# Delta attention: unscaled keys shared by two blocks, new values scaled once more by VectorE

## The chip, the core and the metric

The kernel runs on one NeuronCore of one Trainium2 chip. It is one launch that computes four transformer layers; the time is the device time of the whole launch in microseconds (us), the median over several runs. The engines are TensorE (PE in the profile; PEld is its weight load), VectorE (DVE), ScalarE (ACT), GpSimd (POOL) and SyncE (SP), which issues the DMAs.

## What is computed

The change lies in the last layer's attention, a gated delta rule with 16 key heads, 32 value heads (two per key head) and a head size of 128, for 2 sequences of 512 tokens. The reference works chunk by chunk. For one chunk and one value head, with a state S (128x128), cumulated gate g and its last value g_last:

```
v_new = v_i - kcd_i @ S
out_i = (q_i * exp(g_i)) @ S + a_i @ v_new
S     = S * exp(g_last) + (k_i * exp(g_last - g_i)).T @ v_new
```

Then the output is multiplied by silu(z), normed, and projected. The factor exp(g_last - g_i) is one number per token and value head; it may be applied to the key row or to the row of v_new. The key itself is the same for both value heads of a key head.

## The kernel before, in words

The function `delta_and_looked_up` (from L1782) holds this attention. A chunk is 128 tokens, so a sequence has CH = 4 chunks. One iteration of the main loop works on one block w of W = 64: one key head h = w // 4 and one chunk c = w % 4, for the 2 sequences and the 2 value heads at once, so PR = 4 blocks of 128x128 side by side (B = 2 sequences, VPK = 2 value heads each). The state goes on from chunk to chunk inside a head, so the blocks of a head are serial, and the last chunk of a head (c = 3) grows no state.

The loop is a software pipeline written out by hand, one program per engine, with semaphores between them. In iteration w each engine works on several blocks:

- PE (L2341 to L2377), in this order: `recall(w-1)` (keys times state), `make_scores(w+2)`, `ask(w-1)`, `turn_values(w+2)`, `solve(w-1)`, then background part 0, `join_a(w)`, `grow_state(w-1)` (L2213), `close_a(w)`, `answer(w-1)` (L2205), `join_b(w)`, part 1, `close_b(w)`, `turn_out(w-2)` (L2222), part 2, `turn_keys(w+2)` (L2101), `join_c(w)`, `project_out(w-2)` (L2232), part 3, `close_c(w)`. The parts are projections of the next heads: iterations with c = 2 and c = 3 have three qkv parts (L2043), c = 0 has two, c = 1 has four z parts (L2053).
- ACT (L2519 to L2555): `make_decay` and `grow` (two exponentials, L2409 and L2415), `new_values(w-1)` (L2447: four scaled copies from PSUM, one per block, to `v_new`), copies of the inverse's pieces, squares, and last `make_keys(w+2)` (L2421: four copies from PSUM to `k_row`, each scaled by the gate K_LEFT of its block). In c = 1 it also does four silus of the next head, so that the exponential's table has to be loaded anew before the next `make_decay`.
- DVE (L2815 to L2851): `make_low(w+2)`, `make_right(w-1)`, `make_v0(w+2)` (L2650), `widen(w)`, `make_at(w+2)` (L2641), `close_wa(w)` (L2671), `make_qg(w+2)` (L2655), `copy_za(w)`, `carry(w-1)` (L2704), `gated(w-1)` (L2693, writes `xf`), the convolution of a later head (L2618, L2621), `copy_z_half`, `reduce(w-1)`, `add_out(w-2)` (L2725).
- POOL (L2601 to L2606): `substitute(w+2)` (L2577: the forward substitution of 16x16 blocks as 28 tiny multiplies and adds, L2585 to L2598), then `root(w-1)` (L2567) and `normed(w-1)` (L2573, writes `xnorm`).
- SP (L2008 to L2027): loads, `spread(w+2)` (v0 through DRAM to `l16`, what POOL's substitution starts from: L1970, L1976, L1984) and `gather(w+1)`.

The product that grows the state, L2218, takes per block its own scaled key `k_row[:, w % 4, r, :]` as the stationary operand and `v_new[:, r, :]`, 128 columns, as the moving one. `turn_out(w-2)` and `grow_state` share a PSUM bank (BR), `turn_values` and `turn_keys` another (BT), which is why `turn_values(w)` waits for the k_row copies of w - 1 (L2094).

Of the kernel before, what the change touches and what calls it, by code (L numbers as in the profile page):

```python
# [13 lines left out]
ALU = mybir.AluOpType  # L14
# [3 lines left out]
P = 128  # L18
# [3 lines left out]
TT = N // P  # L22
# [1759 lines left out]
def delta_and_looked_up(nc, ps, d, x, xn, norm, looked_up):  # L1782
# [19 lines left out]
    with Stage(nc, "a3") as s:  # L1802
# [49 lines left out]
        wa, wb, za, tb = (s.buf(n, [P, PR, HP]) for n in ("wa", "wb", "za", "tb"))  # L1852
        wc, z_half, t_half = (s.buf(n, [P, PR, P // 2]) for n in ("wc", "z_half", "t_half"))
        inv = s.buf("inv", [P, 2, PR, P])
        at, qg, v_row, k_row = (s.buf(n, [P, 4, PR, P]) for n in ("at", "qg", "v_row", "k_row"))
        state, rest, v_new = (s.buf(n, [P, PR, P]) for n in ("state", "rest", "v_new"))
        xf, sq, xnorm, out_t = (s.buf(n, [P, PR, P]) for n in ("xf", "sq", "xnorm", "out_t"))
        sums, var, rstd = s.buf("sums", [P, PR]), s.buf("var", [P, PR]), s.buf("rstd", [P, PR])

# [6 lines left out]
        def sems(*names):  # L1866
            return [s.sem(n) for n in names]
# [21 lines left out]
        (xf_ready, sq_ready, var_ready, rstd_ready, xnorm_ready, ot_psum, ot_ready, y_psum, added) = sems(  # L1889
            "xf_ready", "sq_ready", "var_ready", "rstd_ready", "xnorm_ready", "ot_psum",  # L1890
            "ot_ready", "y_psum", "added")
        (stored,) = sems("stored")
        (up_ready, silu_ready, gated_ready, down_done, f_added) = sems(
            "f_up_ready", "f_silu_ready", "f_gated_ready", "f_down_done", "f_added")
# [15 lines left out]
        def bank(n):  # L1910
            return ps[:, n, :].rearrange("p (r t) -> p r t", r=PR)
# [42 lines left out]
        with nc.Block() as block:  # L1954
# [82 lines left out]
            def _(pe):  # L2037
# [53 lines left out]

                def turn_values(w):
                    if w >= 1:
                        pe.wait_ge(krow_ready, PR * w)  # L2094
                    if w % CH == 0:
                        pe.wait_ge(qkv_ready, 4 * (w // CH) + 3 if w else 4)
                    for r in range(PR):
                        mm = pe.transpose(bank(BT)[:, r, :], chunk(w, 2 + r % VPK, r // VPK), ident[:, :])
                    mm.then_inc(vrow_psum, 1)
# [113 lines left out]
                def grow_state(w):  # L2213
                    if w % CH == CH - 1:
                        return
                    pe.wait_ge(vnew_ready, PR * (w + 1))
                    for r in range(PR):
                        mm = pe.matmul(bank(BR)[:, r, :], k_row[:, w % 4, r, :], v_new[:, r, :],  # L2218
                                       start=True, stop=True)
                    mm.then_inc(ds_psum, 1)  # L2220

                def turn_out(w):  # L2222
# [157 lines left out]
            def _(act):  # L2380
# [39 lines left out]

                def make_keys(w):  # L2421
                    act.wait_ge(krow_psum, w + 1)
                    for r in range(PR):
                        act.activation(k_row[:, w % 4, r, :], bank(BT)[:, r // VPK, :], ACT.Copy,
                                       scale=gate(K_LEFT, w, r)).then_inc(krow_ready, 1)

                def copy_tb(w):
                    act.wait_ge(a_psum, w + 1)
# [180 lines left out]
            def _(dve):  # L2609
# [74 lines left out]
                def make_right(w):  # L2684
# [4 lines left out]
                    for r in range(PR):  # L2689
                        dve.scalar_tensor_tensor(rest[:, r, :], bank(BR)[:, r, :], gate(K_NEG, w, r),  # L2690
                                                 v_row[:, w % 4, r, :], ALU.mult, ALU.add).then_inc(rest_ready, 1)

                def gated(w):  # L2693
                    dve.wait_ge(o_psum, w + 1)
                    if w % CH == 0:
                        dve.wait_ge(zs_ready, 4 * (w // CH) + 4)
                    if w >= 1:
                        dve.wait_ge(sq_ready, PR * w)
                        dve.wait_ge(xnorm_ready, w)
                    dve.scalar_tensor_tensor(xf[:, :, :].rearrange("p (b v) t -> p b (v t)", b=B),  # L2700
                                             bank(BO).rearrange("p (b v) t -> p b (v t)", b=B), float(P) ** -0.5,
                                             zs[:, w // CH % 2, w % CH::CH, :], ALU.mult, ALU.mult).then_inc(xf_ready, 1)
# [112 lines left out]
                for w in range(W + 2):  # L2815
                    late = w % CH == 2
                    if made(w + 2):
                        make_low(w + 2)
                    if made(w - 1):
                        make_right(w - 1)  # L2820
                    if made(w + 2):
                        make_v0(w + 2)
                    if made(w):
                        widen(w)
                    if made(w + 2):
                        make_at(w + 2)
                    if made(w):
                        close_wa(w)
                    if made(w + 2):
                        make_qg(w + 2)  # L2830
                    if made(w):
                        copy_za(w)
                    if made(w - 1):
                        carry(w - 1)
                        gated(w - 1)
                    conv(w, 0)
                    if late:
                        conv(w, 1)
                        conv(w, 2)
                    if made(w):  # L2840
                        copy_z_half(w)
                    if not late:
                        conv(w, 1)
                        conv(w, 2)
                        conv(w, 3)
                    if made(w - 1):
                        reduce(w - 1)
                    if late:
                        conv(w, 3)
                    if made(w - 2):  # L2850
                        add_out(w - 2)  # L2851
# [174 lines left out]
```

## Time and profile before

| what | value |
|---|---|
| median of 3 runs | 2029.11 us (2028.65 to 2031.85) |
| the profiled execution, its own time | 2028.85 us |
| span in that profile | 2027.0 us |
| PE busy over the span | 1843.1 us (91%) |
| DVE, ACT, POOL busy | 1287.5, 995.4, 1077.0 us |

The profile's page gives the busy time of each engine. A busy PE is not PE at its peak, since the ends of matmuls are modelled; and an engine with much idle time can still be in the path that sets the end. The main loop of the delta attention runs from about 950 us to the end. The chain of waits (followed back from the last instruction) names, piece by piece, what held the end; the view of waits adds up who waited for whom; the timeline shows single instructions with the idle time ahead of them in brackets.

### The profile page before, as it was taken

What the parts mean: (1) busy time and instruction counts of PE and PEld (TensorE: products, weight loads), DVE (VectorE), ACT (ScalarE), POOL (GpSimd) and SP (SyncE); (2) the same over time, 40 slices, a digit from 0 to 9 for tenths busy, and PEclk for the clock granted to TensorE, in tenths of its full rate; (3) what the DMA queues carried; (4) which work ended last, traced back from release to release, by engine and by line L of the source; (5) the groups of instructions that cost most, each with busy time, mean ns of one, the idle gap of its engine ahead of it and who ended that gap; (6) DMA issues with size and microseconds to landing.
All of it is one profiled execution on the core that took longest, in us unless ns stands there. A gap on an engine that the chain in (4) does not pass through costs nothing.

```text
span 2027.0 us, 45825 instructions
## 1 busy us (share of the span) xinstructions
PE 1843.1 (91%) x16855; PEld 1191.5 (59%) x16855; DVE 1287.5 (64%) x2490; ACT 995.4 (49%) x2433; POOL 1077.0 (53%) x2259
## 2 busy tenths in 40 slices
PE   7799997877899896898999999999999999999987
PEld 5422564432243574346777777777777777677775
DVE  2544564695578533627777777777777777777752
ACT  2375232215321452525656656665666566566643
POOL 0521222224100340126887787887878888888873
PEclk7899998998999796999999999999999999999999
DMA  6035422110010632202222222222222222222221
GB/s 157 1 116 156 108 46 53 52 62 1 1 44 7 176 116 88 40 14 56 53 53 64 64 54 54 64 63 55 49 60 54 53 64 64 54 53 64 44 45 32
DMA packets 231181, 124.42 MB, mean 61 GB/s; under 512 B 141360, under 2 KB 210513, under 8 KB 230705
## 3 DMA queue, kind: packets, MB, share of 16 engines
q1 hardware_dynamic: 225008, 111.20, 22.1%
q0 software_dynamic: 5952, 10.29, 2.2%
q8 instruction: 137, 2.24, 0.5%
q14 instruction: 84, 0.68, 0.1%
HBM read 87.94 MB, written 39.74 MB: 63 GB/s over the span
## 4 chain that ended last, share of the span: by engine, by line
PE 23%; POOL 20%; issue 6%; SPq 4%; ACT 3%; DMA 2%; DVE 2%; POOLq 0%; DVEq 0%; ACTq 0%
POOL a_term L2591 8%; POOL a_z L2595 8%; PE ps L2043 5%; PE ps L2053 3%; PE ps L2242 3%; SPq L1976 2%; POOL a_rstd L2567 2%; POOL a_xnorm L2573 2%; PE ps L2273 2%; DMA a_l<-a_v_dram 1%; SPq L1984 1%; PE ps L2229 1%; PE ps L2160 1%; PE ps L2209 1%; PE ps L2283 1%
## 5 line engine op out<-in xcount | busy, mean ns | idle before, releaser
L2591 POOL TENSOR_TENSOR a_term<-a_z,a_l 32x14 f32<-32x14 f32 (+6 forms) x896 | 342.8, 383 | 70.3
L2595 POOL TENSOR_TENSOR a_z<-a_z,a_term 32x14 f32<-32x14 f32 (+6 forms) x896 | 339.6, 379 | 70.2
L2621 DVE SCALAR_TENSOR_TENSOR a_qkv<-a_raw,a_taps,a_qkv 128x1024 f32<-128x1024 f32 x192 | 247.1, 1287 | 6.1
L2043 PE MATMUL ps<-all_xn,a_w_qkv 128*128 128x512 f32 x512 | 246.7, 607 | 0.0
L390 POOL DMA_INDIRECT f_rows<-a_row,a_slots x32 | 35.4, 1105 | 184.6 <-DVE a_of_tile L380 139.2
L2242 PE MATMUL ps<-a_out_t,a_w_out 128*128 128x256 f32 x512 | 130.7, 399 | 1.9 <-ACT a_out_t L2465 1.7
L2043 PEld LDWEIGHTS ps<-all_xn,a_w_qkv 128*128 128x128 f32 x512 | 89.2, 193 | 69.1 <-issue 67.3
L2386 ACT ACTIVATE a_raw<-ps 128x512 f32<-128x512 f32 x128 | 76.4, 598 | 108.2 <-PE ps L2043 107.5
L2053 PE MATMUL ps<-a_w_z,all_xn 128*128 128x256 f32 x512 | 122.6, 383 | 0.0
L2585 POOL COPY a_z<-a_l 32x256 f32<-32x256 f32 x64 | 27.1, 423 | 154.6 <-DMA a_l<-a_v_dram 154.4
L850 POOL DMA_INDIRECT f_sums<-a_y,a_xs x23 | 36.1, 1568 | 136.3 <-ACT a_y L799 133.4
L2242 PEld LDWEIGHTS ps<-a_out_t,a_w_out 128*128 128x128 f32 x512 | 93.8, 193 | 17.8 <-ACT a_out_t L2465 2.3
L2700 DVE SCALAR_TENSOR_TENSOR a_xf<-ps,a_zs 128x512 f32<-128x512 f32 x64 | 44.2, 690 | 91.0 <-POOL a_xnorm L2573 65.5
L2053 PEld LDWEIGHTS ps<-a_w_z,all_xn 128*128 128x128 f32 x512 | 93.6, 190 | 12.7 <-issue 1.2
L2650 DVE SCALAR_TENSOR_TENSOR a_v<-ps,a_gates,a_decay 128x128 f32<-128x128 f32 x256 | 71.6, 340 | 43.0 <-ACT a_decay L2409 43.0
L2450 ACT ACTIVATE a_v_new<-ps,a_gates 128x128 f32<-128x128 f32 x256 | 72.9, 367 | 45.7 <-PE ps L2192 45.7
L2635 DVE SCALAR_TENSOR_TENSOR a_low<-a_gc_rows,a_gates,a_floor 128x128 f32<-128x128 f32 x256 | 87.9, 403 | 1.6 <-DMA a_gc_rows<-a_g_dram 1.6
L630 PE MATMUL ps<-a_w,a_xt 128*128 x184 | 86.6, 593 | 0.6 <-ACT a_xt L779 0.6
L2567 POOL TENSOR_TENSOR a_rstd<-a_var,a_half 128x4 f32<-128x4 f32 x64 | 68.7, 1073 | 22.1 <-DVE a_var L2719 22.1
L772 ACT ACTIVATE a_probs<-ps 128x512 f32<-128x512 f32 x128 | 66.1, 602 | 23.9 <-PE ps L593 23.9
L2445 ACT ACTIVATE a_inv<-ps 128x512 f32<-128x512 f32 x64 | 38.3, 598 | 76.9 <-PE ps L2169 76.9
L2209 PE MATMUL ps<-a_v_new,a_at 128*128 128x128 f32 x512 | 74.8, 290 | 1.2 <-ACT a_v_new L2450 1.2
(331 smaller groups left out, 4304.7 us busy)
## 6 DMA issues: line engine op xcount, KB each, us to landing
a_gc_rows<-a_g_dram SPq DMA_DIRECT2D x64, 256.0 KB, 4.8
a_v_dram<-a_v SPq DMA_DIRECT2D x64, 256.0 KB
a_w<-in_f_w SPq DMA_DIRECT2D x24, 512.0 KB, 4.5
a_w_qkv<-in_a_w SPq DMA_DIRECT2D x16, 512.0 KB, 3.9
a_t_dram<-a_z SPq DMA_DIRECT2D x512, 8.0 KB
a_w_z<-in_a_w SPq DMA_DIRECT2D x16, 256.0 KB, 2.9
a_w_out<-in_a_wo SPq DMA_DIRECT2D x16, 256.0 KB, 3.1
a_v_off<-a_v SPq DMA_DIRECT2D x256, 4.0 KB
```

Source lines behind the costliest of these rows:

```text
L630: mm = pe.matmul(ps[:, bank + i % 2, :], xt[:, i % 2, k, :], w[:, bass.ds(e, 1), first + k * FF:first + (k + 1) * FF], start=k == 0, stop= ...
L2043: mm = pe.matmul(ps[:, to, :], w_qkv[:, k, mt * P:(mt + 1) * P], xn[:, k, b * T:(b + 1) * T], start=k == 0, stop=k == KC - 1)
L2053: mm = pe.matmul(ps[:, to, i * 256:(i + 1) * 256], xn[:, k, tt * P:(tt + 1) * P], w_z[:, k, :], start=k == 0, stop=k == KC - 1)
L2209: mm = pe.matmul(bank(BO)[:, r, :], at[:, w % 4, r, :], v_new[:, r, :], start=w % CH == 0 and r == 0, stop=r == PR - 1)
L2242: mm = pe.matmul(bank(BO)[:, B * m:B * (m + 1), :], w_out[:, v, m * P:(m + 1) * P], out_t[:, v::VPK, :], start=v == 0, stop=v == VPK - 1)
L2386: act.activation(raw[:, mt, b, TAPS - 1:], ps[:, of, :], ACT.Copy).then_inc(raw_ready, 1)
L2450: act.activation(v_new[:, r, :], bank(BR)[:, r, :], ACT.Copy, scale=gate(K_BETA, w, r)).then_inc(vnew_ready, 1)
L2567: pool.tensor_tensor(rstd[:, :], var[:, :], half[:, :], ALU.pow).then_inc(rstd_ready, 1)
L2591: pool.tensor_tensor(term[:, 0:j, j + 1:], z[:, 0:j, j:j + 1].broadcast_to([HP, j, n]), rows[:, j:j + 1, j + 1:].broadcast_to([HP, j, n]), ...
L2595: pool.tensor_tensor(z[:, 0:j, j + 1:], z[:, 0:j, j + 1:], term[:, 0:j, j + 1:], ALU.add).then_inc(sub_step, 1)
L2621: dve.scalar_tensor_tensor(to, rows, tap, to, ALU.mult, ALU.add).then_inc(conv_ready if j == TAPS - 1 else conv_step, 1)
L2635: dve.scalar_tensor_tensor(low[:, r, :], gc_rows[:, w % 2, r, :], gate(K_GC, w, r), floor[:, :], ALU.subtract, ALU.min).then_inc(low_ready, 1)
```

## The change

`make_keys` writes the keys unscaled, one ScalarE copy of 128x256 for the two sequences instead of four scaled copies of 128x128, and `k_row` shrinks from four blocks to two. A new VectorE step `make_left(w-1)` multiplies `v_new` (128x512, SBUF) by the gate K_LEFT, broadcast along each row, into a new buffer `v_left`, for every block but those with c = 3. It stands in VectorE's order between `make_at(w+2)` and `close_wa(w)`. `grow_state` uses the one key of a sequence as stationary operand and two blocks of `v_left`, 256 columns, as moving operand: two matmuls instead of four. It waits for `left_ready` and `krow_ready` as well.

```diff
-        at, qg, v_row, k_row = (s.buf(n, [P, 4, PR, P]) for n in ("at", "qg", "v_row", "k_row"))
-        state, rest, v_new = (s.buf(n, [P, PR, P]) for n in ("state", "rest", "v_new"))
+        at, qg, v_row = (s.buf(n, [P, 4, PR, P]) for n in ("at", "qg", "v_row"))
+        k_row = s.buf("k_row", [P, 4, B, P])
+        state, rest, v_new, v_left = (s.buf(n, [P, PR, P]) for n in ("state", "rest", "v_new", "v_left"))
...
                 def turn_values(w):
                     if w >= 1:
-                        pe.wait_ge(krow_ready, PR * w)
+                        pe.wait_ge(krow_ready, w)
...
                 def grow_state(w):
                     if w % CH == CH - 1:
                         return
+                    pe.wait_ge(krow_ready, w + 1)
                     pe.wait_ge(vnew_ready, PR * (w + 1))
-                    for r in range(PR):
-                        mm = pe.matmul(bank(BR)[:, r, :], k_row[:, w % 4, r, :], v_new[:, r, :],
-                                       start=True, stop=True)
+                    pe.wait_ge(left_ready, grown_before(w + 1))
+                    for b in range(B):
+                        mm = pe.matmul(bank(BR)[:, VPK * b:VPK * (b + 1), :], k_row[:, w % 4, b, :],
+                                       v_left[:, VPK * b:VPK * (b + 1), :], start=True, stop=True)
                     mm.then_inc(ds_psum, 1)
...
                 def make_keys(w):
                     act.wait_ge(krow_psum, w + 1)
-                    for r in range(PR):
-                        act.activation(k_row[:, w % 4, r, :], bank(BT)[:, r // VPK, :], ACT.Copy,
-                                       scale=gate(K_LEFT, w, r)).then_inc(krow_ready, 1)
+                    act.activation(k_row[:, w % 4, :, :], bank(BT)[:, 0:B, :], ACT.Copy).then_inc(krow_ready, 1)
...
+                def make_left(w):
+                    if w % CH == CH - 1:
+                        return
+                    dve.wait_ge(vnew_ready, PR * (w + 1))
+                    left = gates[:, K_LEFT * TT + w % CH:(K_LEFT + 1) * TT:CH, w // CH * VPK:(w // CH + 1) * VPK]
+                    dve.tensor_tensor(v_left[:, :, :].rearrange("p (b v) t -> p b v t", b=B),
+                                      v_new[:, :, :].rearrange("p (b v) t -> p b v t", b=B),
+                                      left.unsqueeze(3).broadcast_to([P, B, VPK, P]), ALU.mult).then_inc(left_ready, 1)
...
                     if made(w + 2):
                         make_at(w + 2)
+                    if made(w - 1):
+                        make_left(w - 1)
                     if made(w):
                         close_wa(w)
```

## Rows read from the trace of the kernel before

**Rows 1.** Iterations c = 2, 3, 0, 1: length, busy us of PE, PEld, DVE, ACT, POOL.

```profile
1293.50:1311.01 17.51, 17.51 (x215) 12.63 (x216) 12.40 (x28) 10.69 (x31) 12.54 (x29) 1.00 0.25 62
1311.01:1328.47 17.46, 17.46 (x216) 12.55 (x215) 14.00 (x32) 9.24 (x29) 14.90 (x36) 1.00 0.21 48
1328.47:1342.61 14.14, 13.72 (x200) 9.98 (x198) 9.97 (x22) 7.67 (x25) 12.14 (x29) 1.00 0.27 46
1342.61:1362.74 20.13, 18.83 (x228) 15.21 (x226) 14.93 (x31) 15.44 (x36) 17.10 (x42) 1.00 0.29 71
```

**Rows 2.** Waits, 1200 to 1950 us: who waited for whom, total us, times, longest.

```profile
POOL a_z L2585 <- DMA a_l<-a_v_dram: 35.1, 21, 3.3
PE ps L2229 <- POOL a_xnorm L2573: 7.0, 11, 1.4
```

**Rows 3.** Chain that ended last, 1275 to 1318 us: start, us, what.

```profile
1293.45 1.03 ACT a_k_row L2424 x4
...
1294.50 1.28 ACT L2409
...
1301.95 2.08 DMA a_l<-a_v_dram
```

**Rows 4.** The same chain, 1352 to 1415 us.

```profile
1368.20 1.09 PE ps L2218 x8
...
1379.35 1.06 PE ps L2180 x4
1380.41 0.86 PE ps L2087 x4
1381.27 0.89 PE ps L2203 x8
...
1404.78 2.50 DMA a_l<-a_v_dram
```

**Rows 5.** Groups by line and form, 952 to 1950 us: busy us, mean ns.

```profile
L2424 ACT ACTIVATE a_k_row<-ps,a_gates 128x128 f32<-128x128 f32 x232 | 66.1, 377 | 0.0
L2419 ACT ACTIVATE a_v_row<-ps 128x512 f32<-128x512 f32 x58 | 33.8, 583 | 0.0
L2441 ACT ACTIVATE a_wc<-ps 64x256 f32<-64x256 f32 x58 | 22.1, 381 | 20.1 <-PE ps L2160 19.3
L2655 DVE TENSOR_TENSOR a_qg<-a_qkv,a_grown 128x512 f32<-128x512 f32 x57 | 40.5, 710 | 0.0
```

**Rows 6.** Timeline, iteration with c = 1, from 1341 us: start, us, engine, line.

```profile
1343.46 0.27 POOL L2595 TENSOR_TENSOR a_z<-a_z,a_term 32x44 f32<-32x44 f32 x1
...
1347.68 0.68 DVE L2641 TENSOR_TENSOR a_at<-ps,a_decay 128x512 f32<-128x512 f32 x1
...
1348.19 1.16 PE L2218 MATMUL ps<-a_v_new,a_k_row 128*128 128x128 f32 x8
1348.34 0.29 DVE L2671 TENSOR_TENSOR a_wa<-ps,a_ident 128x128 f32<-128x128 f32 x1
...
1348.68 0.68 POOL L2595 TENSOR_TENSOR a_z<-a_z,a_term 32x44 f32<-32x44 f32 x1
```

**Rows 7.** Timeline at the end of an iteration with c = 1, from 1284 us: `turn_out`.

```profile
1284.89 0.63 PE L2229 MATMUL ps<-a_ident,a_xnorm 128*128 128x128 f32 x4 [0.37 <-POOL a_xnorm L2573]
```

**Rows 8.** Timeline, iteration with c = 3, from 1300 us.

```profile
1314.35 1.14 ACT L2450 ACTIVATE a_v_new<-ps,a_gates 128x128 f32<-128x128 f32 x4 [1.10 <-PE ps L2192]
...
1316.35 1.16 PE L2218 MATMUL ps<-a_v_new,a_k_row 128*128 128x128 f32 x8
...
1316.49 0.29 DVE L2671 TENSOR_TENSOR a_wa<-ps,a_ident 128x128 f32<-128x128 f32 x1 [1.43 <-PE ps L2115]
```

**Rows 9.** Timeline, iteration with c = 2, from 1284 us.

```profile
1296.89 1.14 ACT L2450 ACTIVATE a_v_new<-ps,a_gates 128x128 f32<-128x128 f32 x4
...
1298.88 0.97 PEld L2218 LDWEIGHTS ps<-a_v_new,a_k_row 128*128 128x128 f32 x8
```

**Rows 10.** Timeline of the last iterations, from 1990 us.

```profile
1999.62 1.16 PE L2218 MATMUL ps<-a_v_new,a_k_row 128*128 128x128 f32 x8 [0.85 <-ACT a_v_new L2450]
```

More of the change, by code:

```diff
@@ L1891, in delta_and_looked_up @@
             "ot_ready", "y_psum", "added")
+        (left_ready,) = sems("left_ready")
         (stored,) = sems("stored")
```

## The prediction

> **What bounds the kernel now.** The change touches only the main loop of the delta attention, so I first cut one head into its four iterations and read the busy times [rows 1]. In c = 2 and c = 3 PE has no idle time at all (17.51 of 17.51, 17.46 of 17.46 us); in c = 0 and c = 1 it idles 0.42 and 1.30 us. So PE has about 1.7 us of slack in a head of 69.24 us. POOL shows less busy time, but its instructions follow one another with short gaps. The view of waits shows its only real idle time: 35.1 us over 750 us, ahead of the substitution, until the DMA of l16 has landed, and also that PE waits 11 times for POOL's xnorm before `turn_out` [rows 2]. The kernel is thus held by PE and POOL in turn, and nothing is gained by relieving one alone.
>
> Next I read how they pass the lead on. The chain of waits leaves PE at the end of c = 1 and goes through ScalarE: the four k_row copies 1.03 us, the load of the exponential's table 1.28, the exponential `decay`, then v0 on DVE, the DMAs, and POOL's substitution [rows 3]. That is **path A**: after it the chain stays on POOL for three iterations and returns to PE at `turn_out` in the next c = 1. In other heads the chain stays on PE through c = 2 and c = 3, with `grow_state` on it (1.09 us), and reaches POOL's substitution only in c = 0, by another landing of the same DMA [rows 4]: **path B**. Both appear side by side in the same trace, so they are almost equally long.
>
> **The change, step by step.** I give each step's effect per head; about 14 heads run in this steady state.
>
> *ScalarE, k_row.* Four copies of 377 ns, started 1.03 us from first to next, or 1.15 to the end of the last, become one of 128x256. A copy of 64x256 takes 381 ns, one of 128x512 takes 583 [rows 5]. 0.38 is nearest in shape; the gain is 1.15 - 0.38 = 0.77 us, between 0.57 and 0.8. It is on the path once a head, ahead of the table load [rows 3]; `make_low` does not hold the load, since the chain runs there through k_row. In the other three iterations ScalarE waits for something else afterwards, so it costs and brings nothing there. What is late next is the DMA landing that POOL waits for, 3.3 us at most [rows 2], so the whole 0.77 is handed to POOL. Path A: -0.77.
>
> *PE, grow_state.* Four matmuls of 128 columns (two passes each, 8 instructions) become two of 256 columns (4 instructions). In place, the 8 take 1.09 us. In the middle of full-size work, 8 of the narrow form take 0.89 and 4 of the wide form 0.86; after small matmuls the wide ones take 1.06 [rows 4]. So the columns bind, not the count: I take 1.06, a gain of 0.03, between 0 and 0.23. Only path B has it, twice: -0.06. The Trainium skill (TensorE: Matmul & The Clock Gate, Back-to-back issue gap) gives a sustained spacing of 81 ns at 128 columns and 131 ns at 512, by which half as many at double width would be clearly cheaper: an estimate from it, 8 x 81 against 4 x at most 131 ns, saves at least 0.12 us a call. By it path B would be 0.24 shorter and the total about 1 us lower. The rows here, 111 and 216 ns, do not agree with it.
>
> *DVE, make_left.* A multiply of 128x512 with both inputs in SBUF: `make_qg` is the same shape and takes 710 ns on average [rows 5], and it holds DVE for some 0.65 us, as `at` does before `close_wa` (1347.68 to 1348.34 [rows 6]). It has to wait for `new_values`, and three things come of it.
>
> (1) In c = 3 v_new is complete at 1315.49, and DVE has 1.43 us of idle time before `close_wa` [rows 8]. The multiply ends near 1316.25, ahead of `grow_state` at 1316.35. Free for PE. In c = 2 v_new is complete at 1298.03 and `grow_state` starts at 1298.88 [rows 9]: 0.11 (the usual step to DVE) + 0.69 + 0.06 gives 1298.9, provided that DVE has finished `at` by 1298.1, which the 0.77 us from k_row takes care of. I take 0.05 of delay; without that cover it would be 0.36.
>
> (2) In c = 1 there is no cover: `at` and `close_wa` stand back to back, v_new has long been there, and `grow_state` starts at 1348.19 [rows 6]. Behind the multiply it starts at 1347.68 + 0.66 + 0.69 + 0.06 = 1349.09, 0.90 later. Queued behind it on PE are `close_a`, `answer`, `join_b`, and all up to `turn_out`; less the 0.03 this is +0.87. `close_wa` goes back 0.65, to 1349.0 to 1349.3, and is done before PE has finished the late `grow_state`. Before `turn_out` PE waits 0.37 us for POOL in the typical head [rows 7], so 0.50 of the 0.87 comes through, against a POOL that does not move. Call this **path C**: it takes path A's start and leaves POOL for DVE and PE one iteration earlier.
>
> (3) POOL shares something with DVE when both work in SBUF. The same POOL add of 32x44 takes 0.27 us alone and 0.68 us when `make_qg` runs over it [rows 6]: +0.41 for one such DVE instruction. `make_left` falls into the substitution in c = 3 and in c = 1, both on path A; in c = 2 it falls where POOL has some 2 us of wait ahead and is free. Per instance between 0 (an add that has just started long enough before) and 0.71 (the whole instruction). Here the Trainium skill (SBUF — State Buffer, SBUF: two separate sides) speaks against the change: a VectorE instruction with two SBUF inputs and a GpSimd one exclude each other for the whole instruction. I weigh that as a rival below; the sum goes by the row.
>
> **The sum per head.** Path A: -0.77 + 0.41 + 0.41 = +0.05. Path C: -0.77 + 0.41 (c = 3) + 0.50 = +0.14. Path B: -0.06 + 0.05 + 0.41 (the multiply of c = 1, in the last substitution before `turn_out`) = +0.40. With a third of the heads on B (5) and the others on the longer of A and C (9): 5 x 0.40 + 9 x 0.14 = 3.3 us. **The last iterations:** the parts end there, the chain passes twice more through k_row (-1.5), and in the last two growing steps the multiply lies bare between `new_values` and `grow_state` (which waits 0.85 for it already [rows 10]); one adds 0.25 because DVE waits for a DMA beside it, the other 0.8. Together -0.5. Sum: +2.8, and I round to +2.5 since some heads will change from B to C. The profiled execution took 2028.85 us, of which the span is 2027.0; it lies 0.26 below the median of 2029.11. 2028.85 + 2.5 = 2031.4, or **2031.6** against the median. A measurement of this kernel can tell 0.2%, 4.1 us, from no change; so the forecast is: no difference, leaning to slower.
>
> **The rivals.**
>
> *R1, slower: POOL is held for the whole multiply.* The mechanism is in (3), its price 0.71 instead of 0.41, twice on path A and once on B: A +0.65, B +0.70, so 14 x 0.67 = +9, less the end's 0.5: 2037.6. It decides from 0.5 us per instance. For it: the skill's rule, and POOL operations over 1 us in the 128x1024 convolutions. Against: 0.41 in the row, since POOL's own idle steps of 0.07 and the add's beginning overlap. Chance 0.15.
>
> *R2, slower: the k_row gain does not arrive.* Place: the turn from c = 1 to c = 2. If after k_row the table load or decay is held by `low`, or the earlier v0 only waits longer in SP's queue or for its DMA, 0.77 is missing and c = 2 loses its cover (+0.31). A +0.82, C +1.2, B +0.7: about +14, 2043. It decides from half of the 0.77. For it: landings of this DMA differ by half a microsecond (2.08 and 2.50 [rows 3, 4]). Against: each piece in the chain follows the one before without a gap. Chance 0.12.
>
> *R3, faster: the multiply costs POOL and PE little.* If the adds slip between, and PE's waits of c = 1 cover 0.87 more often (7.0 us in 11 waits [rows 2] is 0.64 on average): A -0.77, C -0.5, B -0.06 to -0.5 with the 0.23 of `grow_state` twice. 14 x 0.4 = -6: 2023. Chance 0.20.
>
> *R4: only balance.* That each path's changes cancel to within 0.1 us a head, 2029, is inside the forecast. That the change does not do what it says I give no chance of its own: the diff replaces instructions one by one, and none of the new ones can be left out.
>
> **The numbers.** Forecast with R4: 0.53; R1 0.15, R2 0.12, R3 0.20. The forecast's own spread, 2025 to 2038, puts some 0.11 of its 0.53 above 2033.2. Slower: 0.15 + 0.12 + 0.11 = 0.38; faster: 0.20; same: 0.42. The range goes from 2022 (R3) to 2041, near R2, whose upper part is left out.
>
> **What would show it.** Right: one k_row copy of 0.38 us; the idle time before L2585 at the turn to c = 2 down by up to 0.77; in c = 1 PE waits 0.9 us for a_v_left before `grow_state`, and no longer for xnorm before `turn_out`; POOL adds of some 0.7 us at two more places in each head; a `grow_state` of 1.0 to 1.1 us. Wrong: no wait for a_v_left in c = 1, POOL adds unaffected, or heads that are longer than 70 us by more than 0.5.

## The result and the profile after

The kernel after takes 2040.86 us, the median of 10 runs (2036.35 to 2051.86), against 2029.7 for the kernel before: ratio 1.0065 with a 95% interval of 1.0044 to 1.0087, that is 13.2 us more, between 8.9 and 17.7. (The ratios of this document weigh all runs of a set and are not the quotients of its medians; the two medians here differ by 11.2 us. Where an experiment's cost is given in us, it is its ratio taken of the kernel before.) The kernel after once more, in a later set of runs (the last experiment), gave 1.0052 (1.0033 to 1.0071). The forecast was 2031.6 and "no difference, leaning to slower"; it is slower by about five times the +2.5 us forecast. The median lies just inside the stated range, whose upper end of 2041 was drawn near the rival R2 and not from the forecast itself. The profiled execution was the fastest of the ten, 2036.35 us, so the traces below show less of the loss than the medians do.

From the profile's page of the kernel after, span and busy times:

```profile
span 2034.5 us, 45345 instructions
PE 1845.7 (91%) x16663; PEld 1179.5 (58%) x16663; DVE 1321.0 (65%) x2538; ACT 948.8 (47%) x2241; POOL 1092.7 (54%) x2259
```

ScalarE works 46.6 us less than before and DVE 33.5 more, as the diff says. POOL, whose code is not touched, is busy 15.7 us longer: the first sign that something holds it.

The four iterations of one head, windows of the kernel after; length, then busy us of PE, PEld, DVE, ACT, POOL, the granted clock of PE, DMA share and GB/s. They answer to [rows 1], each from PE's `make_scores` to the next: c = 2, 3, 0, then the c = 1 ahead of this c = 2 and the one behind this c = 0.

```profile
1298.19:1315.66 17.47, 17.47 (x210) 12.33 (x211) 13.11 (x29) 9.98 (x27) 13.08 (x30) 1.00 0.25 67
1315.66:1333.11 17.45, 17.45 (x212) 12.26 (x210) 14.62 (x33) 8.50 (x26) 15.04 (x34) 1.00 0.26 47
1333.11:1347.25 14.14, 13.72 (x200) 9.97 (x198) 9.68 (x22) 7.03 (x23) 11.49 (x27) 1.00 0.25 40
1277.54:1298.19 20.65, 18.87 (x225) 14.92 (x223) 15.45 (x32) 14.69 (x33) 17.62 (x42) 1.00 0.28 70
1347.25:1369.02 21.77, 18.88 (x224) 14.93 (x222) 15.88 (x32) 14.68 (x33) 18.59 (x44) 1.00 0.27 65
```

c = 2, 3 and 0 are as long as before, to 0.04 us: PE is never idle in the first two, before or after, and the shorter k_row copy can't change them. **What happens to a head happens in c = 1**: the six between 1200 and 1580 us took 20.13 to 20.81 us before and take 20.55 to 21.77 now.

What PE waits for there, timeline of the kernel after from 1276 us (start, us, engine, line; in brackets the idle time ahead and its releaser):

```profile
1278.14 0.38 ACT L2427 ACTIVATE a_k_row<-ps 128x256 f32<-128x256 f32 x1
...
1279.10 0.66 PE L2100 MATMUL ps<-a_ident,a_qkv 128*128 128x128 f32 x4 [0.44 <-DVE all_x L2736]
...
1282.60 0.68 DVE L2643 TENSOR_TENSOR a_at<-ps,a_decay 128x512 f32<-128x512 f32 x1
...
1282.73 0.45 PE L2117 MATMUL ps<-a_t_wide,a_v_off 32*32 32x32 f32 x32 [0.35 <-DVE a_t_wide L2665]
...
1283.20 0.67 DVE L2700 TENSOR_TENSOR a_v_left<-a_v_new,a_gates 128x512 f32<-128x512 f32 x1
1283.28 0.71 POOL L2593 TENSOR_TENSOR a_term<-a_z,a_l 32x44 f32<-32x44 f32 x1
...
1284.02 1.10 PE L2222 MATMUL ps<-a_v_left,a_k_row 128*128 128x256 f32 x4 [0.83 <-DVE a_v_left L2700]
1284.07 0.74 POOL L2597 TENSOR_TENSOR a_z<-a_z,a_term 32x44 f32<-32x44 f32 x1
...
1289.58 0.63 PE L2233 MATMUL ps<-a_ident,a_xnorm 128*128 128x128 f32 x4
```

The reader is to see four things: one k_row copy of 0.38 us; the multiply right behind `at`, and PE idle 0.83 us for it; two POOL steps of 32x44 that take 0.71 and 0.74 instead of 0.27, one beside the new multiply, one beside `make_qg` (this second one took 0.68 before, [rows 6]); and `turn_out` (L2233) that no longer waits for POOL's xnorm. In [rows 7] that wait was 0.37.

Waits, 1200 to 1950 us (total us, times, longest), against [rows 2]:

```profile
POOL a_z L2587 <- DMA a_l<-a_v_dram: 28.1, 24, 2.4
...
PE ps L2222 <- DVE a_v_left L2700: 11.6, 13, 1.2
```

POOL waits less for its DMA, 28.1 us for 35.1, but more often, 24 times for 21; and PE has a new wait of 11.6 us, larger than the 7.0 it had for xnorm (2.2 us, 3 times, now). The chain of waits, 1200 to 1360 us, shows the way that now ends last:

```profile
1201.30 1.05 POOL a_xnorm L2575
...
1208.43 0.69 DVE all_x L2736
1209.11 1.31 DVE a_low L2637 x4
1210.45 0.64 ACT a_decay L2413
1211.45 0.86 DVE a_v L2652 x3
1212.74 0.60 DVE a_at L2643
1213.35 0.61 DVE a_v_left L2700
1214.09 1.10 PE ps L2222 x4
...
1227.13 0.60 ACT a_inv L2447
1228.27 1.13 PE ps L2089 x4
...
1254.03 1.55 DMA a_l<-a_v_dram
```

POOL's xnorm in c = 0, DVE, the multiply, PE through c = 1 and on into c = 2 (from `a_inv` straight to PE, not through k_row), and only from c = 3 on the DMA and POOL. The k_row copy stands nowhere on it in this stretch. Over the 13 heads marked below, the chain passes through k_row at the turn to c = 2 in 8 heads of the kernel before and in 4 of the kernel after (in 4 of its repeat too).

**Where the time is, by stretch.** I mark the first and the fourteenth `turn_out` that stand in a c = 1, 13 heads apart. Timelines of the kernel before, then of the kernel after:

```profile
1005.84 0.63 PE L2229 MATMUL ps<-a_ident,a_xnorm 128*128 128x128 f32 x4 [1.07 <-POOL a_xnorm L2573]
...
1912.36 0.63 PE L2229 MATMUL ps<-a_ident,a_xnorm 128*128 128x128 f32 x4 [1.42 <-POOL a_xnorm L2573]
```

```profile
1009.49 0.63 PE L2233 MATMUL ps<-a_ident,a_xnorm 128*128 128x128 f32 x4
...
1921.53 0.63 PE L2233 MATMUL ps<-a_ident,a_xnorm 128*128 128x128 f32 x4
```

The 13 heads take 906.5 us before and 912.0 after, 0.42 us more each; in the repeat 912.5. So the steady state costs 5.5 to 5.9 us. The rest is at the two ends, which differ from execution to execution: 3.7 and 6.7 us later at the first mark (of the 6.7, 4.6 had arisen before PE's first instruction of this attention), and after the last mark 1.7 less and 4.7 more. The 13 heads are the best measure for a mechanism, the ratio for the whole kernel. I counted both, and also two things in the twelve heads behind the first mark: the mean idle time of PE in c = 1, by the step ahead of which it falls; and POOL's mean idle time ahead of its substitution, by the iteration in which that starts. The column of the 13 heads is one profiled execution each. In those of e1, e2, e4, e5 and e7, but not in the others, the granted clock fell to half for some 3 us inside the 13 heads (in e1, e4 and e5 in one c = 1 near 1357 us, which took 23.0 to 23.6 us), so differences of 2 us in that column decide nothing. The labels are those of the experiments below.

| kernel | ratio | 13 heads | PE idle in c = 1: turn_values / join_a / grow_state / turn_out | POOL idle in c = 2 / 3 / 0 / 1 |
|---|---|---|---|---|
| before | 1 | 906.5 | 0.89 / 0.18 / 0 / 0.48 | 2.52 / 0.10 / 0.19 / 0.31 |
| after | 1.0065 | 912.0 | 0.59 / 0.34 / 0.84 / 0.22 | 1.70 / 0.52 / 0.30 / 0 |
| e12, after again | 1.0052 | 912.5 | 0.61 / 0.33 / 0.84 / 0.27 | 1.87 / 0.49 / 0.32 / 0 |
| e1, no multiply | 0.9994 | 906.1 | 0.53 / 0.32 / 0 / 0.66 | 2.14 / 0.88 / 0.41 / 0.07 |
| e10, e1 in answer-first order | 0.9990 | 904.4 | 0.55 / 0.32 / 0 / 0.71 | 2.08 / 0.84 / 0.39 / 0.01 |
| e2, before + unread multiply | 1.0061 | 922.1 | 1.15 / 0.31 / 0 / 0.89 | 2.34 / 0.20 / 0.16 / 0.24 |
| e8, the same from PSUM | 1.0011 | 910.4 | 1.02 / 0.28 / 0 / 0.57 | 2.76 / 0.18 / 0.21 / 0.24 |
| e11, e2's multiply in c = 1 only | 1.0026 | 915.3 | 0.97 / 0.28 / 0 / 0.91 | 2.89 / 0.11 / 0.07 / 0.16 |
| e3, after, multiply from PSUM | 1.0047 | 910.5 | 0.54 / 0.33 / 0.84 / 0.22 | 2.28 / 0.71 / 0.42 / 0.08 |
| e4, after, answer first | 1.0034 | 913.5 | 0.66 / 0.30 / 0 / 1.10 | 1.90 / 0.49 / 0.24 / 0 |
| e5, both | 0.9996 | 906.5 | 0.48 / 0.33 / 0 / 0.83 | 2.12 / 0.83 / 0.43 / 0.03 |
| e6, before, answer first | 1.0025 | 906.7 | 0.89 / 0.21 / 0 / 0.54 | 2.38 / 0.15 / 0.22 / 0.38 |
| e7, e3 with the multiply before `at` | 1.0050 | 905.6 | 0.50 / 0.33 / 0.22 / 0.37 | 1.98 / 1.20 / 0.53 / 0.10 |
| e9, e7, answer first | 0.9986 | 907.1 | 0.56 / 0.37 / 0 / 0.74 | 2.07 / 1.01 / 0.39 / 0.05 |

### The profile page after: what moved, and what is told of

Same layout as the page of the kernel before. It is cut to its first block, busy times and chain, and to the rows that moved or that the text cites. A ratio compares the mean times of both kernels' runs of the same rounds, so it can differ in the third digit from the quotient of the medians.

```text
span 2034.5 us, 45345 instructions
## 1 busy us (share of the span) xinstructions
PE 1845.7 (91%) x16663; PEld 1179.5 (58%) x16663; DVE 1321.0 (65%) x2538; ACT 948.8 (47%) x2241; POOL 1092.7 (54%) x2259
## 4 chain that ended last, share of the span: by engine, by line
PE 27%; POOL 12%; DVE 8%; issue 5%; SPq 3%; ACT 3%; DMA 2%; DVEq 0%; POOLq 0%; ACTq 0%
PE ps L2045 5%; POOL a_term L2593 5%; POOL a_z L2597 5%; PE ps L2055 4%; PE ps L2246 3%; DVE a_qkv L2623 2%; PE ps L2211 2%; SPq L1978 2%; PE ps L2222 2%; PE ps L2277 2%; DVE a_low L2637 1%; DVE a_v L2652 1%; DMA a_l<-a_v_dram 1%; PE ps L2194 1%; PE ps L2233 1%
## 5 line engine op out<-in xcount | busy, mean ns | idle before, releaser
L2593 POOL TENSOR_TENSOR a_term<-a_z,a_l 32x14 f32<-32x14 f32 (+6 forms) x896 | 350.4, 391 | 70.3
L2460 ACT ACTIVATE a_sq<-a_xf 128x128 f32<-128x128 f32 x256 | 75.1, 297 | 0.0
```

Of the source, the lines that this page charges most:

```text
L2460: act.activation(sq[:, r, :], xf[:, r, :], ACT.Square, accum_out=sums[:, r:r + 1]).then_inc(sq_ready, 1)
L2593: pool.tensor_tensor(term[:, 0:j, j + 1:], z[:, 0:j, j:j + 1].broadcast_to([HP, j, n]), rows[:, j:j + 1, j + 1:].broadcast_to([HP, j, n]), ...
```

## The experiments

Theory: PE and POOL are two paths of the same length that meet at `turn_out` in c = 1, and the change lengthens both, PE's by a bare wait for v_left and POOL's by the time in which the multiply holds it, while k_row's gain is on neither (e2 corrects this last point). Rivals: the gain is real and the multiply eats it; or only one of the two costs counts.

**The gain's half alone (e1).** No `make_left`; `grow_state` multiplies `v_new` itself, so the factor exp(g_last - g_i) is left out of the state.

```diff
-                    pe.wait_ge(left_ready, grown_before(w + 1))
...
-                                       v_left[:, VPK * b:VPK * (b + 1), :], start=True, stop=True)
+                                       v_new[:, VPK * b:VPK * (b + 1), :], start=True, stop=True)
...
-                    if made(w - 1):
-                        make_left(w - 1)
```

> The changed kernel without its multiply: one unscaled key copy, the wide matmul takes v_new itself (so the factor exp(g_last - g) is left out of the state). Theory L (a combined path: PE enters c = 2 through a_zs, not through k_row, so the 0.77 us of the copies are mostly not on the path; the 13 us come from the multiply, which makes PE wait 0.9 us in c = 1 and holds POOL): 1 to 4 us below the kernel before. Rival G (the key copies were really on the path in every head and the gain of 0.77 us is there, only more than eaten up by the multiply): 8 to 11 us below.

Measured: 0.9994 (0.9978 to 1.0009), so 1.2 us below, inside the theory's 1 to 4, and the rival's 8 to 11 lie outside the interval. No gain that can be told, though four copies had become one and eight matmul instructions four. Waits of this run, 1200 to 1950 us:

```profile
POOL a_z L2586 <- DMA a_l<-a_v_dram: 40.0, 26, 3.6
...
PE ps L2232 <- POOL a_xnorm L2574: 7.7, 11, 1.8
```

POOL waits longer and more often than before (35.1 us, 21 times), and the table says where. In c = 2 v0 and `at` do stand 0.76 us earlier against PE's work. But the next one, in c = 3, then waits 0.88 us instead of 0.10 for its own DMA, whose source v0 is made by PE's side, and PE has no slack in c = 2 and c = 3 [rows 1]. POOL's starts, counted from PE's `make_scores` of c = 2 (means of the twelve heads), show it at once: the substitution of c = 2 starts at 10.56 us before and at 9.73 in e1, the next one, of c = 3, at 27.31 and 27.24. Of 0.83 us only 0.07 is left: what was saved is returned one iteration later. The chain passes through k_row in 1 of the 13 heads of e1, against 8 before. In c = 1 PE waits 0.36 less for the keys and 0.32 more before `join_a` and `turn_out`.

**The cost's half alone (e2, e8).** The kernel before, with the multiply in its place on DVE, and nobody reads `v_left`. In e2 it reads v_new from SBUF, as the change does; in e8 its first input is a PSUM bank of the same shape (the second part of the diff is e8 against e2).

```diff
+                    if made(w - 1):
+                        make_left(w - 1)
                     if made(w):
                         close_wa(w)
...
-                                      v_new[:, :, :].rearrange("p (b v) t -> p b v t", b=B),
+                                      bank(BK).rearrange("p (b v) t -> p b v t", b=B),
```

> The kernel before plus the multiply in its place on VectorE; nobody reads v_left and PE does not wait for it (close_wa behind it still goes back). It has the cost on VectorE and GpSimd alone. Theory L: two POOL stalls of 0.4 us a head, +3 to +7 us against before, about half of the change. Rival C (contention between VectorE and GpSimd is the whole cost): +12 us or more. Rival W (PE's wait before grow_state is the whole cost): within 2 us of before.

> The kernel before plus a multiply that nobody reads, like the one that cost 12 us, in the same place and with the same wait, but its first input is the scores in PSUM instead of v_new in SBUF. Same time on VectorE, one SBUF input instead of two. Theory L2: the 12 us go to 0 to +2 us. Rival O: +8 to +13 us.

Measured: e2 1.0061 (1.0037 to 1.0085), 922.1 us for 13 heads; e8 1.0011 (0.9993 to 1.0029), 910.4. By the ratios an unread multiply costs as much as the whole change, 12.4 us, at the lower edge of the rival C that I had set against my own +3 to +7; and most of it (10.2 of the 12.4 us, and 11.7 of the 15.6 in the 13 heads) disappears with one input in PSUM, at the same duration of the multiply. Timeline of e2, then of e8, the multiply in c = 1 and the POOL step beside it:

```profile
1282.60 0.29 POOL L2596 TENSOR_TENSOR a_z<-a_z,a_term 32x50 f32<-32x50 f32 x1
...
1282.90 0.68 DVE L2699 TENSOR_TENSOR a_v_left<-a_v_new,a_gates 128x512 f32<-128x512 f32 x1
1282.96 0.72 POOL L2592 TENSOR_TENSOR a_term<-a_z,a_l 32x44 f32<-32x44 f32 x1
```

```profile
1281.57 0.68 DVE L2699 TENSOR_TENSOR a_v_left<-ps,a_gates 128x512 f32<-128x512 f32 x1
1281.64 0.28 POOL L2592 TENSOR_TENSOR a_term<-a_z,a_l 32x50 f32<-32x50 f32 x1
```

0.68 us on DVE in both; POOL's step (32x44 and 32x50, which alone take 0.25 to 0.29) takes 0.72 beside the one and 0.28 beside the other. Most of the cost is thus not DVE's time but what the multiply takes from POOL. What e8 still shows in its 13 heads, 3.9 us, was not followed up; `close_wa` stands later there as well.

k_row's gain is not wholly without use, though. POOL's substitution of c = 3 starts, on the same scale as above, at 27.31 us before, at 28.07 in e2 (at 27.52 in e11 below, without the multiplies of c = 2 and c = 3) and at 27.27 in the kernel after. With the multiply that runs beside the substitution begun in c = 2, the next one comes 0.76 late, and with the shorter k_row it is in time again. It agrees that the 13 heads of the kernel after, 912.0, are 10.1 us shorter than e2's although PE waits for v_left there (0.78 a head); the ratios of the two, 1.0065 and 1.0061, do not show it, so over the whole kernel this stays open.

**One of the three multiplies (e11).** As e2, but only in the iteration with c = 1.

```diff
-                    if w % CH == CH - 1:
+                    if w % CH != 0:
                         return
```

> The kernel before with the unread multiply from SBUF, only in the iteration in which c = 0's values are scaled (it runs in c = 1, beside the substitution that ends at turn_out). With it in all three iterations the time was 1.0061 [1.0037, 1.0085]. Theory (POOL's adds are held 0.4 to 0.5 us per multiply on POOL's path, once a head here instead of twice or three times): a third to a half of it, +4 to +7 us. Rival 1 (only this one counts, since it is the last ahead of turn_out): +12. Rival 2 (only those of c = 2 and c = 3 count; in c = 1 POOL's substitution has slack, or closing w_a late is what costs): 0 to +2.

Measured: 1.0026 (1.0012 to 1.0039), +5.3 us, 915.3 for 13 heads: 8.8 of the 15.6 us that all three cost in this stretch, by the ratios 5.3 of 12.4. So the dose counts, and the multiply of c = 1, the last ahead of `turn_out`, bears about half. The substitution that is running when c = 1 begins takes, from its first to its last instruction, 15.13 us instead of 14.57.

**From PSUM in the changed kernel (e3).** beta is taken into the gate once, and the multiply reads the same bank that `new_values` reads.

```diff
+                dve.tensor_tensor(kind(K_LEFT), kind(K_LEFT), kind(K_BETA), ALU.mult).then_inc(g_step, 1)
...
-                                      v_new[:, :, :].rearrange("p (b v) t -> p b v t", b=B),
+                                      bank(BR).rearrange("p (b v) t -> p b v t", b=B),
```

> The changed kernel, but the multiply takes its first input from PSUM (the solve's result times a gate that already holds beta times exp(g_last - g)) instead of v_new in SBUF; same place, same wait for v_new, same size. It then has one SBUF input, like make_at, over which POOL was hardly late. Theory L: the POOL stalls at the multiply go, PE's wait of 0.9 us in c = 1 stays: +5 to +9 us against before. Rival C: back to before or below it (0 to -3). Rival W: +12 us, no change.

Measured: 1.0047 (1.0032 to 1.0063). Waits of e3, 1200 to 1950 us:

```profile
PE ps L2222 <- DVE a_v_left L2700: 10.4, 12, 1.2
...
PE ps L2233 <- POOL a_xnorm L2575: 1.8, 3, 0.7
```

POOL is free again and early, and PE is late at `turn_out` by itself: it waits for v_left in every head and for xnorm in three. With POOL relieved, the kernel still loses 9.5 us by its ratio, just over the +5 to +9 expected, and 4.0 us in the 13 heads. That this is PE's bare wait is shown by e5 below, which covers the wait and loses nothing.

**Answer first (e4).** PE's order becomes join_a, answer, close_a, grow_state, join_b, so that two steps which don't need v_left cover the multiply.

```diff
-                    if made(w - 1):
-                        grow_state(w - 1)
+                    if made(w - 1):
+                        answer(w - 1)
                     if made(w):
                         close_a(w)
-                    if made(w - 1):
-                        answer(w - 1)
+                    if made(w - 1):
+                        grow_state(w - 1)
```

> The changed kernel with another order on PE: join_a, answer, close_a, grow_state, join_b. answer (1.09 us) needs v_new alone and covers the multiply; it also covers the wait of 0.42 us for close_wa in c = 0. Theory L: PE's wait in c = 1 goes, POOL's stalls stay: 0 to +5 us against before. Rival C: +12 us. Rival W: 2 to 8 us below before, since 0.42 us a head of PE's idle time goes as well.

Measured: 1.0034 (1.002 to 1.0049), 6.9 us, where 0 to +5 had been expected. Timeline of e4 in c = 1:

```profile
1281.02 1.16 PE L2211 MATMUL ps<-a_v_new,a_at 128*128 128x128 f32 x8
...
1282.76 1.13 PE L2222 MATMUL ps<-a_v_left,a_k_row 128*128 128x256 f32 x4
...
1287.47 0.63 PE L2233 MATMUL ps<-a_ident,a_xnorm 128*128 128x128 f32 x4 [0.91 <-POOL a_xnorm L2575]
```

The wait for v_left is gone, and 0.91 us of waiting for POOL stands in its place: the other path, held by the multiply, is now the long one.

**Both (e5).**

> Both remedies at once: the multiply reads PSUM, and PE does answer ahead of close_a and grow_state. Theory L2 (after the first four runs: POOL is held about 0.5 us by each multiply with two SBUF inputs, which alone explains the 12 us of the unread multiply; PE's bare wait of 0.9 us in c = 1 is a second, separate cost of up to 9 us on a path that does not pass k_row; each alone is as large as both together, because the slowest path counts): both gone, so 0 to -6 us against before. Rival O (the cost is VectorE's own time: any instruction of 0.67 us in that place costs it): +5 us or more still.

Measured: 0.9996 (0.998 to 1.0013). Timeline of e5:

```profile
1280.16 0.67 DVE L2700 TENSOR_TENSOR a_v_left<-ps,a_gates 128x512 f32<-128x512 f32 x1
1280.23 0.25 POOL L2593 TENSOR_TENSOR a_term<-a_z,a_l 32x44 f32<-32x44 f32 x1
...
1285.94 0.63 PE L2233 MATMUL ps<-a_ident,a_xnorm 128*128 128x128 f32 x4 [0.33 <-POOL a_xnorm L2575]
```

Each remedy alone leaves 7 to 9.5 us (their intervals overlap that of the kernel after, so the ratios alone don't prove either of them a help); the two together leave nothing. That is how two parallel paths behave, and not how two costs in a row do.

**The same order without the change (e6), and the multiply ahead of `at` (e7, e9).** e6 is the kernel before with e4's order; e7 is e3 with `make_left` ahead of `make_at`; e9 is e7 with e4's order.

> The kernel before with only PE's order changed (join_a, answer, close_a, grow_state, join_b), which covers PE's wait of 0.42 us for close_wa in c = 0. Theory L2 (POOL's path is as long as PE's and is untouched): 0 to -3 us. Rival P (the kernel before is bound by PE alone, so its idle time counts in full): -5 to -6 us.

> The multiply from PSUM, and ahead of make_at instead of behind it; PE's order as in the changed kernel. In c = 1 it should end 0.66 us earlier, so that PE's wait before grow_state shrinks from 0.9 to 0.25 us. Theory L2: 0 to +4 us against before, 5 us or more below the multiply from PSUM behind make_at (which was 9.5 above). Rival O: no better than that one, +8 to +11 us.

> The kernel after with all remedies: multiply from PSUM with a premultiplied factor, issued ahead of make_at, and PE's order answer, close_a, grow_state. Theory (two costs on parallel paths: POOL held by the multiply's SBUF inputs, and PE's bare wait in c = 1; both gone here): 2024 to 2030 us, within 0.2% of before, as the run with the two remedies (0.9996). Rival (placing the multiply first delays at, the state's narrow matmuls and with them the substitution's input, a third path of its own, as the run with only the early PSUM multiply suggests, 1.0050): 2034 us or more. Sign to look at in the profile: from at of c = 2 to v0, and POOL's wait for a_l, each longer by up to 0.7 us under the rival.

Measured: e6 1.0025 (1.0009 to 1.0041), e7 1.0050 (1.0025 to 1.0075), e9 0.9986 (0.9971 to 1.0001). The first two are misses: 0 to -3 us had been expected of e6 and 0 to +4 of e7, and e7's 10 us are what rival O (any instruction of that length in that place costs it) had foretold. In the profiled execution of e7 the 13 heads take 905.6 us and PE waits 0.22 for v_left instead of 0.84, as hoped, and this execution took 2027.87 us; but only three of the eight runs lie there (2025.6 to 2028.5), the others at 2035.4 to 2042.7, and none of those was profiled. The mean granted clock parts the two groups: 0.955 to 0.959 in the three, 0.949 to 0.953 in the five. So rival O fits the ratio and not the profile; what lowers the clock in one execution and not in the next is left open. e6's heads take 906.7, as before, and by its ratio it is 5 us slower all the same. e9 has the lowest ratio of the kernels that keep the change, and can't be told from the kernel before or from e5.

**k_row's gain again, with answer first (e10).**

This is e1, whose state leaves the factor out, in e4's order.

> The gain's half (single key copy, wide matmuls, no multiply; the state leaves out the factor left) with PE's order answer, close_a, grow_state. Theory (the key copy's 0.77 us is never on the slowest path, whatever PE's order): between the kernel before (1.000) and the kernel before with that order (1.0025), so 2028 to 2034 us. Rival (the order frees POOL's path, and then k_row's saving shows): 2020 to 2024 us, 0.3% below before.

Measured: 0.9990 (0.9977 to 1.0003), 904.4 us for 13 heads. Not the 0.3% of the rival: by the ratio it is 2 us of the 10.8 that 14 times 0.77 would be, and POOL again waits 0.84 us in c = 3. That it lies below e6, whose order it has, speaks for some of the gain; its interval, which holds 1.000, leaves this open.

**The kernel after once more (e12).**

> The kernel after unchanged, on the same chip as the three others, to have its median and interval beside theirs and a second profiled execution. Theory: 1.0044 to 1.0087 again, +9 to +18 us, PE in c = 1 waiting some 0.8 us for a_v_left, POOL's period in c = 3 17.1 to 17.2 us. Rival (the difference was that chip's or that set of runs'): within 0.2% of before.

Measured: 1.0052 (1.0033 to 1.0071), with the same idle times in c = 1. The loss is the kernel's, not that of one set of runs.

## Why the prediction was wrong, point by point

**The single steps were right.** One k_row copy of 0.38 us; next to nothing from the wide matmul (c = 2 takes 17.48 us on average, 17.50 before; the forecast was 0.03 for each call); `grow_state` in c = 1 later by 0.84 of a forecast 0.87; no wait for v_left in c = 3; POOL steps of 0.7 us at the places named.

**Two terms failed: "so the whole 0.77 is handed to POOL. Path A: -0.77", and "Together -0.5" for the last iterations.** The heads were to cost 3.3 us in 14, or 3.1 in 13; the 13 took 5.5 and 5.9 more. The rest of the measured 13.2 us, some 7.5, lies outside them, where I had -0.5. By size the second term is the larger miss.

**Why the 0.77 did not arrive.** It was handed over for one iteration and no longer. I had asked what is late next and answered with the landing in c = 2, which did have 2.5 us of idle time; the landing behind it, in c = 3, had 0.10, and it hangs on PE, which never waits there. [rows 1] show that PE is idle in neither c = 2 nor c = 3, and this was enough to see that POOL can't start the substitution of c = 3 more than 0.10 us earlier. An earlier start could pay only for what holds POOL before that point, the multiply of c = 3, and the rest of the gain lapses; the multiply of c = 1 comes behind that point and has to be paid in full. With this limit and 0.53 us for each multiply (the paragraph on POOL's stall), path A becomes -0.10 (of -0.77 + 0.53 no more than 0.10 can be kept) plus 0.53: +0.43 a head, 5.6 us in 13, against 5.5 and 5.9 measured. That is an estimate made afterwards from e1, e2 and e11. Striking the -0.77 out altogether would give path A +0.82, nearly twice the measured cost of a head, and its total of 2038.6 would fit the measured time only because the ends were wrong as well. R2 (2043, chance 0.12) came nearest in its sum, by luck: it denied the gain at another place (the table load, `low` or the queue ahead of the landing in c = 2), the gain did arrive there (POOL's idle time in c = 2 fell from 2.52 to 1.70 us), and R2's +14 was to come from the heads.

**Path C was given a start that it doesn't have.** It took path A's start and so A's -0.77 in full. The chain of the kernel after enters PE from `a_inv`, stays on it through c = 2 and, in one head of the two, c = 3, then goes over the DMA to POOL, DVE, the multiply and PE again. Such a path has PE's bare wait and no gain. I composed paths from the chain of before; a change that moves the balance makes new combinations of their pieces.

**POOL's stall was undersized, and R1's rule was nearer than the price I took.** I took 0.41 us for each multiply from [rows 6]. The substitution that is running when c = 1 begins grew from 14.57 to 15.10 us, first to last instruction, so 0.53, beyond R1's point of 0.5; that of c = 2 to 3 took 14.75 against 14.22 in e1, which has the same k_row and no multiply, again 0.53. The rows show a POOL step that begins 0.08 us after the multiply (1283.28 against 1283.20) and ends 0.12 after it (1283.99 against 1283.87). By the Trainium skill (SBUF — State Buffer, SBUF: two separate sides) a VectorE operation with two SBUF inputs and a GpSimd one that reads SBUF take the shared ports in turns, each for its whole instruction; both the end behind the multiply's end and the absence of any stall with a PSUM input (e3, e5, e8) agree with it. I gave the rule 0.15 because the excess of one add was 0.41 rather than 0.71, but that excess is counted from the start of the add, not from when it could have started.

**"Less the 0.37 of cover" was right for a POOL that doesn't move, and POOL moved.** In the table, PE's idle time in c = 1 of the kernel after is 1.99 us for 1.55 before: +0.84 for v_left, -0.30 at `turn_values`, +0.16 at `join_a`, -0.26 at `turn_out`. That is +0.44 a head, where the forecast had 0.14 for nine heads and 0.40 for five. The signs that I had named for being right came, near enough; they could not tell 0.24 us a head from 0.44.

**The ends.** The forecast gave them -0.5 us, for the last iterations alone. The pairs of profiles show +3.7 and +6.7 before the first mark and -1.7 and +4.7 behind the last, so +2.0 and +11.4 together. More than half of the measured 13 us thus lies outside the 13 heads. I had no term for the start, and none for the clock, which the last section takes up. No experiment was made on the ends; that the two remedies together bring the whole kernel back to 0.9996 says only that this part is gone as well when both costs are.

## What to carry to other kernels

A gain on a path that has slack a few steps later is returned there: follow an earlier start through every following wait of the whole period, and stop where the engine that feeds one of them is never idle. Up to that point it can pay for another delay on the same path, as it did here for one of two stalls; beyond it, nothing is left. When two paths tie, test both halves of a change by themselves and both remedies together: here each remedy alone left 7 to 9.5 us and the two together left nothing. A VectorE operation beside a busy GpSimd is cheap or dear by where its inputs lie: with one of them in PSUM the same 0.68 us cost 2.2 us instead of 12.4, the first of them not told from nothing.

## What the runs showed of the hardware that was not expected

A POOL operation of 0.25 to 0.29 us took 0.71 to 0.72 beside a VectorE multiply of two SBUF inputs and 0.25 to 0.28 beside the same multiply with one input in PSUM. That an input's place decides this, and not the length of the VectorE instruction, I had not counted on.

In the profiles of the kernel before, the kernel after and its repeat the granted clock of PE is 1.00 in all of 1010 to 1910 us, but it falls at both ends of the loop, and not in the same places in each execution. From 900 us to the end it is at its lower level for 14 us in all before, 21 after and 35 in the repeat. In e1 it also fell once in between, at 1355 us, as PE came out of a wait of 1.82 us for xnorm. Windows of the kernel after, then of the kernel before (length, busy, clock; columns as above), and the wait ahead of it in the kernel after:

```profile
930.00:935.00 5.00, 1.66 (x35) 1.38 (x36) 2.42 (x5) 1.94 (x3) 4.14 (x12) 0.65 0.61 162
935.00:940.00 5.00, 5.00 (x87) 4.04 (x86) 2.49 (x5) 1.98 (x4) 2.22 (x9) 0.67 0.30 76
```

```profile
930.00:935.00 5.00, 3.59 (x121) 3.21 (x120) 3.34 (x9) 3.67 (x7) 4.08 (x12) 1.00 0.72 205
```

```profile
932.70 0.65 PE L2117 MATMUL ps<-a_t_wide,a_v_off 32*32 32x32 f32 x32 [3.79 <-DVE a_t_wide L2665]
933.99 2.04 PE L2222 MATMUL ps<-a_v_left,a_k_row 128*128 128x256 f32 x4 [0.64 <-DVE a_v_left L2700]
```

PE had been idle 3.79 us (1.41 at this place before), and then the clock was in part at its lower level, 1.2 GHz: the same `grow_state` took 2.04 us instead of 1.10. In the repeat of the kernel after the clock is at that level from 2015 to 2025 us, with PE busy nearly throughout (in the 5 us ahead it was busy for 3.34):

```profile
2015.00:2020.00 5.00, 4.62 (x107) 4.14 (x108) 2.75 (x8) 0.91 (x3) 0.00 (x0) 0.50 0.02 3
2020.00:2025.00 5.00, 5.00 (x19) 3.67 (x18) 0.24 (x2) 2.24 (x11) 2.04 (x2) 0.50 0.00 0
```

Over the runs of the kernel after the mean clock of the whole span goes with the time, from 0.955 at 2036.35 us to 0.950 at 2051.86. Over whole sets of runs its mean is 0.9577, 0.9582 and 0.9566 for the kernel before, and 0.9543 and 0.9541 for the kernel after, 0.9537 for e3 and 0.9535 for e7, but 0.9579 for e5 and for e8. As an estimate from these, 0.003 of 2035 us is 6 us of PE time, and no more than that can be lost by it, which is of the size of the loss at the ends. But e1, with a mean of 0.9552, loses nothing. So part of the spread, and perhaps part of the loss at the ends, goes with the clock. That is read from profiles and was not tested; whether the change makes a lower clock more likely stays open.
